# Two sets of operand sums change engines in the score rounds of a cross-attention kernel

## The chip, the cores and the metric

The kernel runs on one core of a Trainium2 chip. The metric is the device time of one launch in microseconds (us). PE is TensorE, DVE is VectorE, ACT is ScalarE, POOL is GpSimd, SP is SyncE (here it only issues DMA transfers).

## The reference

```python
def reference(x, ctx, mask, Wq, Wk, Wv, Wo, gamma, beta, gate):   # x 8x1024x1024, ctx 8x64x1024
    a = layer_norm(ctx, gamma, beta)
    Q = split_heads(x @ Wq.T)            # 16 heads of 64
    K = split_heads(a @ Wk.T)
    V = split_heads(a @ Wv.T)
    s = where(mask, Q @ K.T * 64 ** -0.5, -inf)   # 8 x 16 x 1024 x 64
    out = merge_heads(softmax(s) @ V) @ Wo.T
    return x + tanh(gate) * out
```

Everything is float32.

## The kernel before

Since a batch has only 64 keys, Wq and K are multiplied first: for every batch b the kernel builds M[b], a 1024x1024 matrix (model dimension by 16 heads times 64 keys), in scratch DRAM, so that all scores of the batch are x[b] times M[b]. That is the first stage (about 186 us). The second stage, the score rounds, does these products; the third, the output rounds, does softmax, the product with V, and the product with Wo.

A score round n (0 to 15) is one half batch, 512 rows of x, against M[n // 2], 1024x1024. The product is split once by a seven-product scheme in the manner of Strassen and Winograd: the left operand A (the transposed x) is cut into four quadrants, the right operand B (M) into four quadrants, and seven products of sums of quadrants, P1, P5, P6, P3, P7, P2, P4 in this order, give the result. A *step* s is one such product: n = s // 7, k = s % 7. Steps 0 to 111 are score rounds, 112 to 223 output rounds. A step is two groups of 12 matmuls (every float32 operand is split into a high and a low float32r part, and high*low, low*high, high*high are added), plus one small mask matmul for each group of P1.

Around each step:

- **Sums of A.** P5, P6, P3 and P7 have a sum or difference of A quadrants on the left; P1, P2, P4 take a quadrant as it is. `sum_a(n, k)` makes such a sum, 128x1024 elements, from `xq` (the loaded quadrants of x) into `a_sum` (two buffers). Before the change it is a POOL instruction (line 552), and the semaphore `sum_made` counts them: 4 a round, 64 in the score rounds.
- **Split of A.** `split_a_hi(s)` is an ACT cast into `a_ring` (L656), `split_a_lo(s)` the DVE subtraction behind it (L849). PE's step s waits for the latter (`a_lo_made`). `a_ring` has two slots, so the cast for step s+1 starts when step s-1 is done (`item_done`).
- **Sums of B.** Once a batch (every 14 steps) the seven B operands in `parts` are refilled for the next batch, two pieces (q = 0 to 13) for each product, while the second round of the batch is running: `refill_step` puts pieces q at steps 8 to 19 counted from the first step of the batch's round pair. `sum_b(rnd, k)` makes the four B sums in place in `b_raw` (three 128x2048 buffers), for P5, P6, P7, P4, after pieces 1, 3, 5 and 11. Before the change it is a DVE instruction (L883), 128x2048 elements, counted by `t_made`: 4 a batch, 32 in all. The cast of the next piece (`split_b_hi`, ACT, L680) waits for it; the DVE subtraction `split_b_lo` (L862) follows the cast.
- **Results.** `copy_out` (ACT, L691) copies the first product into an output quadrant from PSUM, `add_out` (DVE, L905) adds the others.

Each engine takes its instructions strictly in the order in which the program issues them; semaphores alone join the engines. DVE's order in step s is: `add_out` of step s-1, `split_a_lo(s+1)`, the refill pieces of step s with their B sum, and at the ninth step of every batch the small mask instruction (L844). POOL has nothing else to do in these rounds, so it does each A sum as soon as its inputs and its buffer are free.

Of the kernel before, what the change touches and what calls it, by code (L numbers as in the profile page):

```python
# [5 lines left out]
ALU = mybir.AluOpType  # L6
# [13 lines left out]
def xattn_kernel(nc, x, x_t, ctx_x, mask, wq_b, wk_t, wv_t, wo_t, gamma, beta, gate, out):  # L20
    rows, D = x.shape
    B, S = mask.shape
# [20 lines left out]
    with ExitStack() as ctx:  # L43
# [20 lines left out]
        b_raw = at("b_raw", 112, [P, 3, HC, HD])  # L64
        a_sum = at("a_sum", 136, [P, 2, HC, 2, P])
# [73 lines left out]
        m_stored = sems("m_stored", 3)  # L139
# [80 lines left out]
        def a_quad(n, r, half):  # L220
            return x_pair(2 * n + half)[:, :, :, r, :]

        def a_source(n, k):
            if k in A_QUAD:
                return a_quad(n, *A_QUAD[k])
            return a_sum[:, A_SUM[k]]

        def wait_quad(eng, n, half):
            if n < ROUNDS:
                y = 2 * n + half  # L230
                eng.wait_ge(x_in[y % 3], 16 * (y // 3 + 1))
            else:
                eng.wait_ge(o_made, NC * (n - ROUNDS) + HC * (half + 1))
# [14 lines left out]
        def refills(s):  # L248
            return [(rnd, q) for rnd in range(B + 1) for q in range(14) if refill_step(rnd, q) == s]
# [259 lines left out]
        @block.gpsimd  # L509
        def _(pool):  # L510
            nc.gpsimd.memset(ident[:], 0.0).then_inc(ident_zero, 1)
            pool.wait_ge(ident_zero, 1)
            nc.gpsimd.affine_select(out=ident[:], in_=ident[:], compare_op=ALU.not_equal, fill=1.0, base=0,
                                    pattern=[[-1, P]], channel_multiplier=1).then_inc(ident_made, 1)
            nc.gpsimd.memset(neg_half[:], -0.5).then_inc(ident_zero, 1)
            nc.gpsimd.memset(ones_row[:].bitcast(F32), 0.0).then_inc(rows_zeroed, 1)
            pool.wait_ge(ident_zero, 2)
            for i in range(CT):
                pool.wait_ge(var_added, i + 1)
                nc.gpsimd.tensor_tensor(rstd[:, i:i + 1], var_eps[:, i:i + 1], neg_half[:], ALU.pow  # L520
                                        ).then_inc(rstd_made, 1)
            pool.wait_ge(rows_zeroed, 1)
            nc.gpsimd.memset(ones_row[0:1, :].bitcast(F32), 1.0).then_inc(rows_zeroed, 1)
            for w in range(ITEMS):
                hi, lo = w_ring[:, w % 6, 0, :], w_ring[:, w % 6, 1, :]
                pool.wait_ge(w_hi_made, w + 1)
                nc.gpsimd.tensor_tensor(lo, w_raw[:, w % 4, :], hi.bitcast(F32), ALU.subtract).then_inc(w_lo_made, 1)

            def sum_a(n, k):
                if k == P5:  # L530
                    wait_quad(pool, n, 0)
                    wait_quad(pool, n, 1)
                    if n > 0:
                        pool.wait_ge(a_lo_made, 7 * (n - 1) + P3 + 1)
                    else:
                        pool.wait_ge(m_stored[2], 16 * 5)
                        pool.wait_ge(m_first_stored[0], 16)
                    one, two, op = a_quad(n, 1, 0), a_quad(n, 1, 1), ALU.add
                elif k == P6:
                    pool.wait_ge(sum_made, 4 * n + 1)  # L540
                    if n > 0:
                        pool.wait_ge(a_lo_made, 7 * (n - 1) + P7 + 1)
                    one, two, op = a_sum[:, 0], a_quad(n, 0, 0), ALU.subtract
                elif k == P3:
                    pool.wait_ge(sum_made, 4 * n + 2)
                    pool.wait_ge(a_lo_made, 7 * n + P5 + 1)
                    one, two, op = a_quad(n, 0, 1), a_sum[:, 1], ALU.subtract
                else:
                    pool.wait_ge(sum_made, 4 * n + 3)
                    pool.wait_ge(a_lo_made, 7 * n + P6 + 1)  # L550
                    one, two, op = a_quad(n, 0, 0), a_quad(n, 1, 0), ALU.subtract
                nc.gpsimd.tensor_tensor(a_sum[:, A_SUM[k]], one, two, op).then_inc(sum_made, 1)  # L552

            def normalise(u):
                pr = probs[:, u % 4, :].rearrange("p (g s) -> p g s", s=S)
                rec = row_rec[:, u % 2, :].unsqueeze(2).to_broadcast([P, 8, S])
                pool.wait_ge(rec_done, u + 1)
                nc.gpsimd.tensor_tensor(pr, pr, rec, ALU.mult).then_inc(probs_done, 1)  # L558

            sum_a(0, P5)  # L560
            sum_a(0, P6)
            for s in range(STEPS):
                n, k = s // 7, s % 7
                if k == P5:
                    sum_a(n, P3)
                if k == P6:
                    sum_a(n, P7)
                if s == 102:
                    pool.wait_ge(t_made, 4 * B)
                    nc.gpsimd.memset(v_diag[:].bitcast(F32), 0.0).then_inc(v_zeroed, 1)  # L570
                for u in units(2 * s, SUM):
                    normalise(u)
                for u in units(2 * s + 1, SUM):
                    normalise(u)
                if k == P4 and n + 1 < 2 * ROUNDS:
                    sum_a(n + 1, P5)
                    sum_a(n + 1, P6)

# [162 lines left out]
        def _(dve):  # L741
# [104 lines left out]
            def split_a_lo(s):  # L846
                n, k = s // 7, s % 7
                dve.wait_ge(a_hi_made, s + 1)
                nc.vector.tensor_tensor(a_ring[:, s % 2, 1], a_source(n, k), a_ring[:, s % 2, 0].bitcast(F32),  # L849
                                        ALU.subtract).then_inc(a_lo_made, 1)  # L850
# [11 lines left out]
                nc.vector.tensor_tensor(parts[:, k, 1, c:c + 2, :], b_raw[:, B_HOME[k], c:c + 2, :],  # L862
                                        parts[:, k, 0, c:c + 2, :].bitcast(F32), ALU.subtract).then_inc(b_lo_made, 1)

            def sum_b(rnd, k):
                r0, r1, r2 = b_raw[:, 0], b_raw[:, 1], b_raw[:, 2]
                if k == P5:
                    dve.wait_ge(b_in[1], 16 * (rnd + 1))
                    dve.wait_ge(b_lo_made, 14 * rnd + 2)
                    to, one, two = r0, r1, r0  # L870
                elif k == P6:
                    dve.wait_ge(b_in[2], 32 * rnd + 16)
                    dve.wait_ge(b_lo_made, 14 * rnd + 4)
                    to, one, two = r0, r2, r0
                elif k == P7:
                    dve.wait_ge(t_made, 4 * rnd + 1)
                    to, one, two = r1, r2, r1
                else:
                    dve.wait_ge(b_in[2], 32 * rnd + 32)
                    dve.wait_ge(t_made, 4 * rnd + 2)  # L880
                    dve.wait_ge(b_lo_made, 14 * rnd + 12)
                    to, one, two = r2, r2, r0
                nc.vector.tensor_tensor(to, one, two, ALU.subtract).then_inc(t_made, 1)  # L883

            def refill(s):
                for rnd, q in refills(s):
                    split_b_lo(rnd, q)
                    if rnd < B and q in (1, 3, 5, 11):
                        sum_b(rnd, {1: P5, 3: P6, 5: P7, 11: P4}[q])

            def bank_pair(n, k):
                return banks[:, 4:6, :] if k in ON_F else banks[:, 2 * (n % 2):2 * (n % 2) + 2, :]
# [37 lines left out]
            split_a_lo(0)  # L930
            for i in range(CT):
                split_v_lo(1, i)
            for s in range(STEPS):
                rnd = s // 14 + 1
                if s > 0:
                    add_out((s - 1) // 7, (s - 1) % 7)
                if s + 1 < STEPS:
                    split_a_lo(s + 1)
                if s < 104:
                    refill(s)  # L940
                for z in (2 * s, 2 * s + 1):
# [203 lines left out]
```

## Time and profile before

| | us |
|---|---|
| median of 3 runs | 1643.02 (1642.58 to 1645.21) |
| the profiled execution: its own time | 1641.88 |
| its span, first to last instruction | 1640.1 |
| PE busy | 1554.1 (95%) |
| DVE busy | 1173.1 (72%) |
| ACT busy | 860.6 (52%) |
| POOL busy | 536.4 (33%) |

The busy times are sums over the span of one profiled execution. Matmuls overlap in PE's pipeline (one is recorded with 0.39 us and the next starts 0.23 us later), so PE's progress is read from start to start.

### The profile page before, as it was taken

Reading aid. Unit: us, or ns where it says so; the run is one execution under the profiler, and the core shown is the slowest. Engines: PE = TensorE matmul, PEld = TensorE weight load, DVE = VectorE, ACT = ScalarE, POOL = GpSimd, SP = SyncE. Lnnn points to the kernel's source line nnn. Section 1 sums busy time; section 2 is a strip of 40 time slices with the busy share of each in tenths; the row PEclk is TensorE's granted clock in tenths of the full one; section 3 lists DMA queues with packets and bytes.
Section 4 is the critical chain, followed back from the end, with each engine's and each line's share of the span. In section 5 each row is a group of like instructions: output and inputs, shape, how many; then the busy total and the mean of one; then the engine's idle time right before and its main releaser. Section 6 shows DMA issues by size and latency. Waiting matters only on the chain.

```text
span 1640.1 us, 19978 instructions
## 1 busy us (share of the span) xinstructions
PE 1554.1 (95%) x7104; PEld 1254.7 (77%) x7104; DVE 1173.1 (72%) x1216; ACT 860.6 (52%) x1822; POOL 536.4 (33%) x294
## 2 busy tenths in 40 slices
PE   6998799999999999999988999999999999999998
PEld 5755577777777778777766788888888888888887
DVE  8534678686868696968767877777777777777763
ACT  3444344343444444444666766666666666666641
POOL 6322122323232323222323333343433334443331
PEclk9999899999999999999999999999999999999999
DMA  6999862636363635353446544344444434454422
GB/s 232 320 361 377 292 226 103 213 106 210 105 215 106 213 106 202 125 183 128 156 125 183 180 131 135 121 134 137 156 152 132 138 120 133 139 155 149 139 80 90
DMA packets 203841, 275.05 MB, mean 168 GB/s; under 512 B 26464, under 2 KB 92128, under 8 KB 203744
## 3 DMA queue, kind: packets, MB, share of 16 engines
q1 hardware_dynamic: 203744, 273.79, 50.5%
q8 instruction: 57, 0.93, 0.2%
q14 instruction: 40, 0.33, 0.1%
HBM read 164.70 MB, written 109.05 MB: 167 GB/s over the span
## 4 chain that ended last, share of the span: by engine, by line
PE 69%; DVE 14%; issue 6%; DMA 6%; ACT 4%; POOL 0%; SPq 0%; ACTq 0%; DVEq 0%; POOLq 0%
PE banks L966 22%; PE banks L968 21%; PE banks L967 21%; DVE a_ring L849 4%; DVE parts L862 3%; PE banks L1092 3%; DVE c_out L905 2%; DMA w_raw<-wq_b 2%; ACT parts L680 1%; PE banks L1002 1%; DMA w_raw<-wv_t 1%; ACT c_out L691 1%; DMA m_scratch<-m_stage 1%; DVE mask_mov L844 1%; DVE b_raw L883 1%
## 5 line engine op out<-in xcount | busy, mean ns | idle before, releaser
L966 PE MATMUL banks<-parts,a_ring 128*128 128x512 f32 x1792 | 717.6, 400 | 30.7 <-DVE a_ring L849 18.2
L968 PE MATMUL banks<-parts,a_ring 128*128 128x512 f32 x1792 | 703.4, 393 | 0.0
L967 PE MATMUL banks<-parts,a_ring 128*128 128x512 f32 x1792 | 702.8, 392 | 0.0
L966 PEld LDWEIGHTS banks<-parts,a_ring 128*128 128x128 f32 x1792 | 339.7, 190 | 106.0 <-DVE a_ring L849 25.2
L968 PEld LDWEIGHTS banks<-parts,a_ring 128*128 128x128 f32 x1792 | 339.1, 189 | 73.5
L967 PEld LDWEIGHTS banks<-parts,a_ring 128*128 128x128 f32 x1792 | 339.9, 190 | 67.2
L558 POOL TENSOR_TENSOR probs<-probs,row_rec 128x512 f32<-128x512 f32 x128 | 133.8, 1045 | 497.0 <-DVE row_rec L919 497.0
L697 ACT ACTIVATE probs<-probs,neg_max 128x64 f32<-128x64 f32 x1024 | 259.1, 341 | 49.2 <-DVE neg_max L910 49.2
L905 DVE TENSOR_TENSOR c_out<-banks,c_out 128x1024 f32<-128x1024 f32 x160 | 195.1, 1219 | 119.0 <-PE banks L968 114.4
L849 DVE TENSOR_TENSOR a_ring<-a_sum,a_ring 128x1024 fp32r<-128x1024 f32 x128 | 188.4, 1472 | 113.7 <-ACT a_ring L656 112.5
L656 ACT CAST a_ring<-a_sum 128x1024 fp32r<-128x1024 f32 x128 | 134.0, 1047 | 211.6 <-PE banks L968 202.3
L552 POOL TENSOR_TENSOR a_sum<-xq 128x1024 f32<-128x1024 f32 x64 | 167.8, 2622 | 210.0 <-DMA xq<-x_t 105.1
L862 DVE TENSOR_TENSOR parts<-b_raw,parts 128x1024 fp32r<-128x1024 f32 x112 | 186.1, 1676 | 29.4 <-ACT parts L680 29.0
L656 ACT CAST a_ring<-xq 128x1024 fp32r<-128x1024 f32 x96 | 100.5, 1046 | 159.6 <-PE banks L968 159.6
L706 ACT CAST p_parts<-banks 128x512 fp32r<-128x512 f32 x128 | 74.6, 583 | 168.6 <-PE banks L968 114.0
L552 POOL TENSOR_TENSOR a_sum<-xq,a_sum 128x1024 f32<-128x1024 f32 x32 | 77.5, 2423 | 247.2 <-DVE a_ring L849 247.2
L680 ACT CAST parts<-b_raw 128x1024 fp32r<-128x1024 f32 x112 | 115.2, 1047 | 60.2 <-DVE b_raw L883 54.4
L923 DVE TENSOR_TENSOR p_parts<-banks,p_parts 128x512 fp32r<-128x512 f32 x128 | 86.9, 679 | 80.6 <-ACT p_parts L706 80.6
L849 DVE TENSOR_TENSOR a_ring<-xq,a_ring 128x1024 fp32r<-128x1024 f32 x96 | 123.9, 1291 | 2.4 <-ACT a_ring L656 2.4
L915 DVE TENSOR_REDUCE row_sum<-probs 128x8 f32<-128x512 f32 x128 | 87.2, 681 | 19.1 <-ACT probs L697 17.8
L883 DVE TENSOR_TENSOR b_raw<-b_raw 128x2048 f32<-128x2048 f32 x32 | 96.9, 3028 | 3.1 <-DVE parts L862 0.5
L552 POOL TENSOR_TENSOR a_sum<-a_sum,xq 128x1024 f32<-128x1024 f32 x32 | 93.6, 2924 | 11.4 <-DVE a_ring L849 9.4
(74 smaller groups left out, 1266.7 us busy)
## 6 DMA issues: line engine op xcount, KB each, us to landing
xq<-x_t SPq DMA_DIRECT2D x32, 1024.0 KB, 6.8
b_raw<-m_scratch SPq DMA_DIRECT2D x32, 1024.0 KB, 6.3
s_scratch<-c_out SPq DMA_DIRECT2D x64, 512.0 KB, 3.1
probs<-s_scratch SPq DMA_DIRECT2D x128, 256.0 KB, 3.1
c_out<-x SPq DMA_DIRECT2D x64, 512.0 KB, 4.7
out<-c_out SPq DMA_DIRECT2D x64, 512.0 KB, 3.1
m_scratch<-m_stage SPq DMA_DIRECT2D x14, 2048.0 KB, 15.6
w_raw<-wk_t SPq DMA_DIRECT2D x8, 512.0 KB, 7.6
```

The lines of the kernel that those rows point to most:

```text
L552: nc.gpsimd.tensor_tensor(a_sum[:, A_SUM[k]], one, two, op).then_inc(sum_made, 1)
L558: nc.gpsimd.tensor_tensor(pr, pr, rec, ALU.mult).then_inc(probs_done, 1)
L656: nc.scalar.copy(a_ring[:, s % 2, 0], a_source(n, k)).then_inc(a_hi_made, 1)
L680: nc.scalar.copy(parts[:, k, 0, c:c + 2, :], b_raw[:, B_HOME[k], c:c + 2, :]).then_inc(b_hi_made, 1)
L697: last = nc.scalar.activation(probs[:, u % 4, cols], probs[:, u % 4, cols], ACT.Exp, bias=neg_max[:, u % 2, g:g + 1])
L849: nc.vector.tensor_tensor(a_ring[:, s % 2, 1], a_source(n, k), a_ring[:, s % 2, 0].bitcast(F32), ALU.subtract).then_inc(a_lo_made, 1)
L862: nc.vector.tensor_tensor(parts[:, k, 1, c:c + 2, :], b_raw[:, B_HOME[k], c:c + 2, :], parts[:, k, 0, c:c + 2, :].bitcast(F32), ALU.subtra ...
L883: nc.vector.tensor_tensor(to, one, two, ALU.subtract).then_inc(t_made, 1)
L905: nc.vector.tensor_tensor(c_out[:, q], bank_pair(n, k), c_out[:, q], ALU.add).then_inc(added, 1)
L966: pe.matmul(to, wl, mh, start=first, stop=False, skip_group_check=joined)
L967: pe.matmul(to, wh, ml, start=False, stop=False, skip_group_check=joined)
L968: return pe.matmul(to, wh, mh, start=False, stop=last, skip_group_check=joined)
```

## The change

In the score rounds the A sums are issued on VectorE, one at a time inside its steps, and all B sums on GpSimd. In the output rounds (n >= 16) nothing changes: A sums stay on GpSimd. The instructions keep their shapes and operands, and the semaphores their counts; each wait moves with its instruction.

```diff
@@ GpSimd @@
-            sum_a(0, P5)
-            sum_a(0, P6)
+            def refill_sums(s):
+                for rnd, q in refills(s):
+                    if rnd < B and q in (1, 3, 5, 11):
+                        sum_b(rnd, {1: P5, 3: P6, 5: P7, 11: P4}[q])
+
+            refill_sums(-1)
             for s in range(STEPS):
                 n, k = s // 7, s % 7
-                if k == P5:
+                refill_sums(s)
+                if k == P5 and n >= ROUNDS:
                     sum_a(n, P3)
-                if k == P6:
+                if k == P6 and n >= ROUNDS:
                     sum_a(n, P7)
...
-                if k == P4 and n + 1 < 2 * ROUNDS:
+                if k == P4 and ROUNDS <= n + 1 < 2 * ROUNDS:
                     sum_a(n + 1, P5)
                     sum_a(n + 1, P6)
@@ VectorE @@
             def refill(s):
                 for rnd, q in refills(s):
                     split_b_lo(rnd, q)
-                    if rnd < B and q in (1, 3, 5, 11):
-                        sum_b(rnd, {1: P5, 3: P6, 5: P7, 11: P4}[q])
...
+            sum_a(0, P5)
             for s in range(STEPS):
...
                 if s + 1 < STEPS:
                     split_a_lo(s + 1)
+                if k == P1 and n < ROUNDS:
+                    sum_a(n, P6)
+                if k == P5 and n < ROUNDS:
+                    sum_a(n, P3)
+                if k == P6 and n < ROUNDS:
+                    sum_a(n, P7)
+                if k == P4 and n + 1 < ROUNDS:
+                    sum_a(n + 1, P5)
                 if s < 104:
                     refill(s)
```

The GpSimd form of `sum_b` and its waits, which the prediction speaks of:

```python
            def sum_b(rnd, k):
                r0, r1, r2 = b_raw[:, 0], b_raw[:, 1], b_raw[:, 2]
                if k == P5:
                    pool.wait_ge(b_in[1], 16 * (rnd + 1))
                    pool.wait_ge(b_lo_made, 14 * rnd + 2)
                    to, one, two = r0, r1, r0
                elif k == P6:
                    pool.wait_ge(b_in[2], 32 * rnd + 16)
                    pool.wait_ge(b_lo_made, 14 * rnd + 4)
                    to, one, two = r0, r2, r0
                elif k == P7:
                    pool.wait_ge(t_made, 4 * rnd + 1)
                    to, one, two = r1, r2, r1
                else:
                    pool.wait_ge(b_in[2], 32 * rnd + 32)
                    pool.wait_ge(t_made, 4 * rnd + 2)
                    pool.wait_ge(b_lo_made, 14 * rnd + 12)
                    to, one, two = r2, r2, r0
                nc.gpsimd.tensor_tensor(to, one, two, ALU.subtract).then_inc(t_made, 1)
```

VectorE's order from the ninth step of the first round pair on, before (`a_ring` is the split of A, `parts` the split of B, `b_raw` a B sum, `c_out` an `add_out`):

```order
L862 TENSOR_TENSOR parts<-b_raw,parts 128x1024 x2
L883 TENSOR_TENSOR b_raw<-b_raw 128x2048
L849 TENSOR_TENSOR a_ring<-a_sum,a_ring 128x1024
L862 TENSOR_TENSOR parts<-b_raw,parts 128x1024
L844 TENSOR_SCALAR mask_mov<-mask_u 1x512
L849 TENSOR_TENSOR a_ring<-a_sum,a_ring 128x1024
L862 TENSOR_TENSOR parts<-b_raw,parts 128x1024
L883 TENSOR_TENSOR b_raw<-b_raw 128x2048
L905 TENSOR_TENSOR c_out<-banks,c_out 128x1024
L849 TENSOR_TENSOR a_ring<-xq,a_ring 128x1024
```

and after, at the same place (line numbers of the changed kernel: L910 is a sum of A, L875 the split of A, L888 the split of B, L930 an `add_out`):

```order
L910 TENSOR_TENSOR a_sum<-xq,a_sum 128x1024
L888 TENSOR_TENSOR parts<-b_raw,parts 128x1024 x2
L875 TENSOR_TENSOR a_ring<-a_sum,a_ring 128x1024
L910 TENSOR_TENSOR a_sum<-xq 128x1024
L888 TENSOR_TENSOR parts<-b_raw,parts 128x1024
L870 TENSOR_SCALAR mask_mov<-mask_u 1x512
L875 TENSOR_TENSOR a_ring<-a_sum,a_ring 128x1024
L888 TENSOR_TENSOR parts<-b_raw,parts 128x1024
L930 TENSOR_TENSOR c_out<-banks,c_out 128x1024
L875 TENSOR_TENSOR a_ring<-xq,a_ring 128x1024
```

The two 128x2048 B sums are gone from between the splits, and two 128x1024 A sums (for P3 and P7 of the round) stand there.

GpSimd's order from the end of its weight splits on, before:

```order
L527 TENSOR_TENSOR w_ring<-w_raw,w_ring 128x1024 x24
L552 TENSOR_TENSOR a_sum<-xq 128x1024
L552 TENSOR_TENSOR a_sum<-a_sum,xq 128x1024
L552 TENSOR_TENSOR a_sum<-xq,a_sum 128x1024
L552 TENSOR_TENSOR a_sum<-xq 128x1024 x2
```

and after:

```order
L536 TENSOR_TENSOR w_ring<-w_raw,w_ring 128x1024 x24
L573 TENSOR_TENSOR b_raw<-b_raw 128x2048 x32
L596 MEMSET v_diag 128x2048
L579 TENSOR_TENSOR probs<-probs,row_rec 128x512 x11
L553 TENSOR_TENSOR a_sum<-xq 128x1024
```

All 32 B sums stand in a row on GpSimd, with nothing between them but their waits, and the first A sum that GpSimd makes is that of the first output round.

## Rows read from the trace of the kernel before

**Rows 1.** The page, part 1: busy time by engine, share of the span, instructions
```profile
PE 1554.1 (95%) x7104; PEld 1254.7 (77%) x7104; DVE 1173.1 (72%) x1216; ACT 860.6 (52%) x1822; POOL 536.4 (33%) x294
```
**Rows 2.** Windows: start:end, length, busy of each engine (count), clock, DMA share, GB/s
```profile
186.00:249.00 63.00, 53.22 (x195) 42.15 (x196) 45.72 (x31) 23.52 (x24) 19.67 (x7) 0.84 0.68 228
249.00:768.00 519.00, 500.27 (x2187) 408.56 (x2186) 403.63 (x255) 229.53 (x233) 149.69 (x51) 1.00 0.45 153
```
**Rows 3.** Waits of PE, 249 to 768 us: who, us in total, times, longest
```profile
PE banks L966 <- DVE a_ring L849: 18.2, 12, 2.3
PE banks L966 <- issue: 0.6, 1, 0.6
```
**Rows 4.** Timeline of PE: start, duration, instruction [idle before]
```profile
313.01 0.50 PE L966 MATMUL banks<-parts,a_ring 128*128 128x512 f32 x1 [1.19 <-DVE a_ring L849]
...
593.46 0.39 PE L968 MATMUL banks<-parts,a_ring 128*128 128x512 f32 x1
595.43 0.50 PE L966 MATMUL banks<-parts,a_ring 128*128 128x512 f32 x1 [1.58 <-DVE a_ring L849]
...
599.66 0.39 PE L966 MATMUL banks<-parts,a_ring 128*128 128x512 f32 x1
...
606.46 0.39 PE L1079 MATMUL banks<-mask_mov,ones_row 128*128 128x512 f32 x1
```
**Rows 5.** Timeline of DVE, steps 64 to 68
```profile
573.08 1.23 DVE L849 TENSOR_TENSOR a_ring<-a_sum,a_ring 128x1024 fp32r<-128x1024 f32 x1 [4.67 <-ACT a_ring L656]
574.94 4.13 DVE L862 TENSOR_TENSOR parts<-b_raw,parts 128x1024 fp32r<-128x1024 f32 x2 [0.63 <-ACT parts L680]
...
587.49 1.21 DVE L862 TENSOR_TENSOR parts<-b_raw,parts 128x1024 fp32r<-128x1024 f32 x1
588.80 4.31 DVE L883 TENSOR_TENSOR b_raw<-b_raw 128x2048 f32<-128x2048 f32 x1
593.03 1.21 DVE L905 TENSOR_TENSOR c_out<-banks,c_out 128x1024 f32<-128x1024 f32 x1
594.16 1.21 DVE L849 TENSOR_TENSOR a_ring<-xq,a_ring 128x1024 fp32r<-128x1024 f32 x1
```
**Rows 6.** Timeline of POOL in the same steps
```profile
574.45 2.40 POOL L552 TENSOR_TENSOR a_sum<-xq 128x1024 f32<-128x1024 f32 x1 [3.51 <-DVE a_ring L849]
...
587.70 3.26 POOL L552 TENSOR_TENSOR a_sum<-a_sum,xq 128x1024 f32<-128x1024 f32 x1 [1.55 <-DVE a_ring L849]
```
**Rows 7.** Timeline of ACT in the same steps
```profile
577.44 1.05 ACT L656 CAST a_ring<-a_sum 128x1024 fp32r<-128x1024 f32 x1 [1.58 <-PE banks L968]
```
**Rows 8.** Sources L552, L558, L511: count, ns min/median/max, first and last start, shape
```profile
L552 POOL TENSOR_TENSOR a_sum<-xq,a_sum x32: 2377/2398/3192, 196.9 to 1600.0; 128x1024 f32<-128x1024 f32 x32
L558 POOL TENSOR_TENSOR probs<-probs,row_rec x128: 1042/1045/1049, 797.2 to 1577.7; 128x512 f32<-128x512 f32 x128
L511 POOL MEMSET ident<- x1: 205/205/205, 0.7 to 0.7; 128x128 f32 x1
```
**Rows 9.** Timeline of DVE and POOL in the first stage
```profile
22.32 14.83 DVE L767 TENSOR_TENSOR a_parts<-a_scaled_t,a_parts 128x512 fp32r<-128x512 f32 x7
...
24.45 10.95 POOL L527 TENSOR_TENSOR w_ring<-w_raw,w_ring 128x1024 fp32r<-128x1024 f32 x4 [0.29 <-ACT w_ring L589]
```
**Rows 10.** Timeline of POOL, PE and DVE in the first score round
```profile
190.78 2.38 POOL L552 TENSOR_TENSOR a_sum<-xq 128x1024 f32<-128x1024 f32 x1 [32.73 <-DMA xq<-x_t]
...
201.24 0.77 PE L966 MATMUL banks<-parts,a_ring 128*128 128x512 f32 x1 [5.78 <-issue]
...
224.24 0.77 PE L966 MATMUL banks<-parts,a_ring 128*128 128x512 f32 x1 [3.53 <-issue]
...
194.28 2.45 DVE L849 TENSOR_TENSOR a_ring<-a_sum,a_ring 128x1024 fp32r<-128x1024 f32 x1 [5.29 <-ACT a_ring L656]
196.65 4.49 DVE L862 TENSOR_TENSOR parts<-b_raw,parts 128x1024 fp32r<-128x1024 f32 x2
```
**Rows 11.** Timeline of DVE where the score rounds end, last B sum
```profile
789.42 2.29 DVE L883 TENSOR_TENSOR b_raw<-b_raw 128x2048 f32<-128x2048 f32 x1
```

More of the change, by code:

```diff
@@ L226, in a_source, with sum_operands @@
             return a_sum[:, A_SUM[k]]
+        def sum_operands(n, k):
+            if k == P5:
+                return a_quad(n, 1, 0), a_quad(n, 1, 1), ALU.add
+            if k == P6:
+                return a_sum[:, 0], a_quad(n, 0, 0), ALU.subtract
+            if k == P3:
+                return a_quad(n, 0, 1), a_sum[:, 1], ALU.subtract
+            return a_quad(n, 0, 0), a_quad(n, 1, 0), ALU.subtract
         def wait_quad(eng, n, half):
@@ L532, in sum_a @@
                     wait_quad(pool, n, 1)
[L533 to L538, printed above, removed]
+                    pool.wait_ge(sum_made, 4 * n)
+                    pool.wait_ge(a_lo_made, 7 * (n - 1) + P3 + 1)
                 elif k == P6:
                     pool.wait_ge(sum_made, 4 * n + 1)
-                    if n > 0:
-                        pool.wait_ge(a_lo_made, 7 * (n - 1) + P7 + 1)
-                    one, two, op = a_sum[:, 0], a_quad(n, 0, 0), ALU.subtract
+                    pool.wait_ge(a_lo_made, 7 * (n - 1) + P7 + 1)
                 elif k == P3:
@@ L546, in sum_a @@
                     pool.wait_ge(a_lo_made, 7 * n + P5 + 1)
-                    one, two, op = a_quad(n, 0, 1), a_sum[:, 1], ALU.subtract
                 else:
@@ L550, in sum_a, with sum_b @@
                     pool.wait_ge(a_lo_made, 7 * n + P6 + 1)
-                    one, two, op = a_quad(n, 0, 0), a_quad(n, 1, 0), ALU.subtract
-                nc.gpsimd.tensor_tensor(a_sum[:, A_SUM[k]], one, two, op).then_inc(sum_made, 1)
+                nc.gpsimd.tensor_tensor(a_sum[:, A_SUM[k]], *sum_operands(n, k)).then_inc(sum_made, 1)
+            def sum_b(rnd, k):
+                r0, r1, r2 = b_raw[:, 0], b_raw[:, 1], b_raw[:, 2]
+                if k == P5:
+                    pool.wait_ge(b_in[1], 16 * (rnd + 1))
+                    pool.wait_ge(b_lo_made, 14 * rnd + 2)
+                    to, one, two = r0, r1, r0
+                elif k == P6:
+                    pool.wait_ge(b_in[2], 32 * rnd + 16)
+                    pool.wait_ge(b_lo_made, 14 * rnd + 4)
+                    to, one, two = r0, r2, r0
+                elif k == P7:
+                    pool.wait_ge(t_made, 4 * rnd + 1)
+                    to, one, two = r1, r2, r1
+                else:
+                    pool.wait_ge(b_in[2], 32 * rnd + 32)
+                    pool.wait_ge(t_made, 4 * rnd + 2)
+                    pool.wait_ge(b_lo_made, 14 * rnd + 12)
+                    to, one, two = r2, r2, r0
+                nc.gpsimd.tensor_tensor(to, one, two, ALU.subtract).then_inc(t_made, 1)
             def normalise(u):
@@ L863, in split_b_lo, with sum_a @@
                                         parts[:, k, 0, c:c + 2, :].bitcast(F32), ALU.subtract).then_inc(b_lo_made, 1)
-            def sum_b(rnd, k):
-                r0, r1, r2 = b_raw[:, 0], b_raw[:, 1], b_raw[:, 2]
+            def sum_a(n, k):
                 if k == P5:
-                    dve.wait_ge(b_in[1], 16 * (rnd + 1))
-                    dve.wait_ge(b_lo_made, 14 * rnd + 2)
-                    to, one, two = r0, r1, r0
-                elif k == P6:
[L872 to L877, printed above, removed]
-                else:
[L879 to L883, printed above, removed]
+                    wait_quad(dve, n, 0)
+                    wait_quad(dve, n, 1)
+                    if n > 0:
+                        dve.wait_ge(a_lo_made, 7 * (n - 1) + P3 + 1)
+                    else:
+                        dve.wait_ge(m_stored[2], 16 * 5)
+                        dve.wait_ge(m_first_stored[0], 16)
+                elif k == P6:
+                    dve.wait_ge(sum_made, 4 * n + 1)
+                    if n > 0:
+                        dve.wait_ge(a_lo_made, 7 * (n - 1) + P7 + 1)
+                elif k == P3:
+                    dve.wait_ge(sum_made, 4 * n + 2)
+                    dve.wait_ge(a_lo_made, 7 * n + P5 + 1)
+                else:
+                    dve.wait_ge(sum_made, 4 * n + 3)
+                    dve.wait_ge(a_lo_made, 7 * n + P6 + 1)
+                nc.vector.tensor_tensor(a_sum[:, A_SUM[k]], *sum_operands(n, k)).then_inc(sum_made, 1)
             def refill(s):
@@ L932, in _ @@
                 split_v_lo(1, i)
+            sum_a(0, P5)
             for s in range(STEPS):
-                rnd = s // 14 + 1
+                rnd, n, k = s // 14 + 1, s // 7, s % 7
                 if s > 0:
```

## The prediction

> **What bounds the kernel now.** I read the page's busy times first: PE 95%, DVE 72%, POOL 33% [rows 1]. An engine at 33% that takes work from one at 72% sounds like relief, but PE is the bound, so the second view was the windows: what does PE lose, and where? From 249 to 768 us (90 steps, from the ninth step of batch 0 to step 98) the clock is at its upper level, 1.00, throughout [rows 2]. The timeline gives PE's own pace: from 599.66 to 606.46 us lie 30 matmuls, 0.227 us each [rows 4], so a step of 24 is 5.44 us. The waits of that stretch then name the loss: 12 waits of 18.2 us for the DVE split of A, L849, and one of 0.6 us put down to issue [rows 3]. A wait costs a little more than its entry. From the last matmul at 593.46 to the next at 595.43 are 1.97 us where 0.23 is usual, so 1.74 is lost for an entry of 1.58; and from 595.43 to 599.66 are 18 matmuls in 4.23 us instead of 4.08, 0.15 more. That is 0.31 on top of each entry: 18.8 + 13 x 0.31 = 22.8 us in seven periods of 14 steps. All else in these rounds is hidden behind PE.
>
> Then the timelines of DVE and POOL around one stall. DVE's B sum at 588.80 took 4.31 us where the same instruction takes 2.29 when POOL is idle [rows 5, 11]. POOL's A sum started at 587.70 and ended at 590.96 [rows 6]; 593.11 less 2.29 is 590.82. So DVE did nothing until POOL was done. POOL in turn took 3.26 us instead of 2.40, since DVE's split ran until 588.70: both stand still for each other, whole instructions long, whenever both DVE operands are in SBUF. The `add_out` behind it, with PSUM as one operand, kept its 1.21. Behind the long B sum stand `add_out` and the split of A for step 68, which ended at 595.37; PE went on at 595.43. That is one stall of each period. The other kind (1.19, at 313.01 us) is behind the P4 sum, in the same way [rows 4].
>
> **The price of the moved instructions.** A sums on DVE: 128x1024, two SBUF operands, like the split of A: one each 1.14 us (593.03 to 594.16), 1.21 to 1.23 recorded [rows 5]. B sums on POOL: 128x2048 is not in the trace. The nearest row is the 1024 form of the same operation, 2.40 us median; twice that less one fixed part, for which a whole POOL memset of 0.205 us stands: 4.57 [rows 8]. Call it X. From below: a POOL multiply of 512 elements takes 1.045, four of them 4.18. From above: the step from 512 to 1024 is 1.355, so 2.40 + 2 x 1.355 = 5.11. I take 4.57 and keep both ends. Over a batch the pair is then held for 8 x 1.14 + 4 x 4.57 = 27.4 us of sums instead of 8 x 2.40 + 4 x 2.29 = 28.4: no relief in total. What counts is that the longest single block for DVE grows from 2.40 to 4.57.
>
> The Trainium skill, GPSIMD Engine Reference, section 3.1, gives 4497 ns for a `tensor_tensor` add of 2048 float32 on GpSimd and 2293 ns on VectorE; the second agrees with the 2.29 here. With its 4.50 the sum below would come out 1.5 us lower.
>
> **One period after the change, in the times of steps 64 to 69.** Step 66 is due at 593.69 - 2 x 5.44 = 582.81.
>
> Step 64: the split of A starts at 573.08 as before [rows 5], the A sum for P3 at 574.22, the splits of B pieces 0 and 1 at 575.36 and 576.50, the last ending at 577.71 (before: 579.07, since POOL's A sum was in the way). POOL started 0.14 behind such an end (574.31 to 574.45) [rows 5, 6], so the P5 sum of B runs from 577.85 to 577.85 + X. The split of A for step 66 is ready at 578.49, when its cast ends [rows 7], and must wait: a blocked split ends 1.09 behind POOL's end (its 1.23 less the 0.14 by which 590.82 lies ahead of 590.96), PE follows 0.06 later. Step 66 starts at 579.00 + X = 583.57: **stall 0.76**, which was not there before.
>
> Step 66: after the A sum for P7, piece 2, the mask, the split of A and piece 3, DVE reaches about 588.5; the P6 sum of B runs 588.6 to 593.2. The split of A for step 68 is blocked until then and ends at 594.27; due is 583.57 + 0.15 + 10.88 = 594.60. No stall, but only 0.27 of slack; as three blocked waits lie in it, I put 0.15 a period for it.
>
> Step 68: the P7 sum of B waits for nothing but the first sum, so it stands ready behind P6 and takes the pair when that split ends: until 594.27 - 0.14 + 4.57 = 598.70. Piece 4 ends at 599.79, `add_out` and the split of A for step 69 follow 1.14 apart: 602.07, PE at 602.13. Due is 594.60 + 5.44 = 600.04: **stall 2.09**, in the place of the 1.74.
>
> The P4 sum comes at the end of step 73; POOL's two A sums that crowded it are gone, and the split of A that it blocks (for step 75) has 0.6 us to spare by the same chain, so the stall of the second kind goes.
>
> Sum: 0.76 + 2.09 + 2 x 0.15 = 3.15 a period, x7 = 22.1 against 22.8: **-0.7**; slack term 7 x 0.15: **+1.0**. Each X lies once in the first stall and twice more in the second, so one us of X is 21 us of time.
>
> **The first round** [rows 2, 10]. The A sum waits for a load until 190.78. On DVE it takes 1.2 instead of 2.38, and neither the split (2.45) nor the two pieces (4.49) behind it are blocked: 192.0, cast 193.1, split 194.3, A sum 195.5, pieces 197.8. Step 1 starts at 197.9 instead of 201.24, 3.3 earlier. Then P6 and P7 of B, 2 X = 9.1 on POOL, stand in front of step 2's pieces, ending near 211.3, where two DVE sums of 2.29 stood: 2 later than before. PE idles some 5 us there, and after such gaps it starts at the lower of its two levels, 1.2 GHz of 2.4 (0.77 recorded where 0.39 is usual; granted clock 0.84 over the window: 0.16 x 63 = 10 us, about 3.4 for each of three restarts). The restart of 224.24, with 3.53 idle, goes in exchange. I come out even at step 4: **0**, with 3 either way.
>
> **The end.** The last P4 sum of B, 2.29 at 789.42 [rows 11], is X on POOL: ACT's cast behind it, and the first exponentials of the output rounds, start 2.3 later; part of that is slack: **+1.0** (0 to 2.3). Covered at nothing: the later A sum for P7 (it releases a load of x some 7 us later, which is needed 20 us after), and DVE's A sums in steps without a B sum, where ACT's cast leaves DVE idle (4.67) [rows 5].
>
> Total +1.3: 1643.2 for the profiled execution (1641.88 before), 1644.3 for the median (1643.02). It can't be told from no change, which I take as within 0.2%, 3.3 us.
>
> **Rivals.**
> - *X is dearer.* At 4.80, strictly twice 2.40, the periods cost 7 x 3 x 0.23 = 4.8 more: 1649; at 5.11, 1656. It decides from X = 4.67, where the total passes +3.3. For it: nothing in the trace shows a fixed part on a subtract. Chance 0.22.
> - *POOL keeps the pair between P6 and P7*, which have no wait between them: the split for step 68 ends 4.4 later, the stall of 2.09 becomes one of 4.1 with the restart a step earlier, and step 69 goes on 5.44 behind it: 2.4 more a period, 1661. Against it: in the first stage four back-to-back POOL instructions took 10.95 us instead of 4 x 2.40 = 9.6 while DVE had seven splits to do, and only 1.75 us lie between their ends (35.40 and 37.15): most of the splits got in between [rows 9]. Chance 0.06.
> - *X is cheaper* or the blocked splits end earlier than I chain them: below X = 4.35 the total is under -3.3; at 4.18 it is 1.3 - 8.2, 1636. For it: the 512-element row. Chance 0.17.
> - *The first round keeps its gain*: PE stays at the upper clock over the second gap (up to 3.4 less) and step 2 is not later: 1639. Against it: both gaps of this length fell. Chance 0.10.
> - The advice of the Trainium skill, Perfetto Trace Analysis, that moving work between VectorE and GpSimd "might not help" as they share a port, would be no change; the row with 4.31 agrees.
>
> **How the numbers follow.** The forecast has 0.45, with 1641 to 1647.5 as its own range. Slower by over 0.2%: 0.22 + 0.06 and a little of the forecast's edge, 0.29. Faster: 0.17 + 0.10 less edges, 0.25. Same: 0.46. The range leaves out the two ends of X and POOL keeping the pair: 1637.5 to 1653.
>
> **What would show it.** POOL's B sum at 4.5 to 4.6 us when alone. In every period PE stalls before steps 66 and 69 (counted as here), 0.8 and 2.1, each released by the split of A, and none at step 75. DVE's splits of A recorded with up to 5 us beside a POOL B sum. PE's first matmul of step 1 near 198, one at half pace near 211. Wrong would be: stalls before step 68; two B sums of POOL with no DVE instruction ended between them; DVE instructions not stretched by POOL's B sums.

## The result, and the profile after

The changed kernel takes 1656.81 us (median of 4 runs, 1654.07 to 1657.62), the kernel before 1644.12 us beside it (4 runs, 1642.58 to 1645.26). The ratio is 1.0075, 95% interval 1.0057 to 1.0092: slower by 0.75%, above the upper end of the forecast's range. The profiled execution took 1657.14 us with a span of 1655.4, against 1641.88 and 1640.1: 15.3 us more to explain. The kernel before was timed 26 times more beside the experiments, on two other occasions, and spread further there, from 1641.91 to 1651.56; the slowest of those runs still lies below the fastest of the changed kernel.

Page, part 1, of the changed kernel (busy time, share, instructions):

```profile
PE 1564.0 (94%) x7104; PEld 1260.3 (76%) x7104; DVE 1179.9 (71%) x1248; ACT 861.5 (52%) x1822; POOL 509.0 (31%) x262
```

Against [rows 1] nearly nothing is to be seen there except one thing: PE executes the same 7104 matmuls and is busy for 9.9 us longer. Matmuls that wait for an operand are not busy, so some matmuls ran longer. (DVE's time rose by 6.8 us and POOL's fell by 27.4, since the instructions changed places.) The windows say where. They are cut at the first matmul of steps 0, 8, 98 and 112 (start:end, length, busy of PE, PEld, DVE, ACT, POOL with counts, granted clock, DMA share, GB/s), changed kernel. A step of P1 begins with a mask matmul, and step 0 is counted from the one behind it:

```profile
185.70:250.20 64.50, 52.15 (x196) 41.23 (x195) 46.60 (x32) 23.75 (x25) 19.27 (x4) 0.86 0.68 231
250.20:780.10 529.90, 509.56 (x2187) 414.27 (x2186) 409.05 (x279) 230.38 (x233) 131.17 (x27) 0.98 0.44 150
780.10:883.30 103.20, 92.88 (x414) 75.04 (x413) 71.90 (x90) 66.41 (x155) 19.17 (x14) 0.97 0.50 156
```

| stretch | before | after | difference |
|---|---|---|---|
| first stage, to step 0 | 187.0 | 185.7 | -1.3 |
| step 0 to 8 (first round) | 62.3 | 64.5 | +2.2 |
| step 8 to 98 (seven periods) | 519.0 | 529.9 | **+10.9** |
| step 98 to 112 | 100.9 | 103.2 | +2.3 |
| step 112 to the last matmul | 765.9 | 767.1 | +1.2 |

The seven periods hold most of it, and there the granted clock is 0.98 where [rows 2] have 1.00. PE's waits there (who, us in total, times, longest):

```profile
PE banks L1000 <- DVE a_ring L875: 20.3, 14, 2.1
```

[Rows 3] had 18.2 in 12 for the same split of A (L849 then, L875 now) and 0.6 for issue. The waits alone therefore grew by 1.5 us. The rest is in PE's timeline around one of these stalls, before step 69 (start, duration, instruction, idle before it and its releaser):

```profile
606.86 0.39 PE L1002 MATMUL banks<-parts,a_ring 128*128 128x512 f32 x1
609.33 0.50 PE L1000 MATMUL banks<-parts,a_ring 128*128 128x512 f32 x1 [2.08 <-DVE a_ring L875]
609.67 0.40 PE L1001 MATMUL banks<-parts,a_ring 128*128 128x512 f32 x1
609.90 0.59 PE L1002 MATMUL banks<-parts,a_ring 128*128 128x512 f32 x1
610.29 0.63 PE L1000 MATMUL banks<-parts,a_ring 128*128 128x512 f32 x1
...
612.86 0.62 PE L1000 MATMUL banks<-parts,a_ring 128*128 128x512 f32 x1
613.28 0.43 PE L1001 MATMUL banks<-parts,a_ring 128*128 128x512 f32 x1
```

From 606.86 to 609.33 are 2.47 us where 0.23 is usual: a stall of 2.24. Then, from 609.90 on, the matmuls start 0.43 apart instead of 0.23. That is PE's lower clock, 1.2 GHz, and the windows around another such stall (step 13, restart at 281.07) give it outright: 1.00, then 0.50, then 1.00.

```profile
278.80:282.20 3.40, 1.32 (x6) 0.95 (x6) 3.40 (x4) 2.95 (x3) 0.00 (x0) 1.00 0.40 154
282.30:285.60 3.30, 3.30 (x9) 2.53 (x8) 3.30 (x4) 0.00 (x0) 0.00 (x0) 0.50 0.42 158
285.70:343.00 57.30, 57.30 (x254) 47.45 (x254) 38.37 (x29) 24.57 (x25) 8.84 (x2) 1.00 0.52 174
```

Eight matmuls at 0.43 instead of 0.23 cost 1.6 us. It happened behind five of the seven stalls of this kind. Behind the last one (restart at 774.25) and the one at 528.45, of the same length, it did not:

```profile
525.96 0.39 PE L1002 MATMUL banks<-parts,a_ring 128*128 128x512 f32 x1
528.45 0.50 PE L1000 MATMUL banks<-parts,a_ring 128*128 128x512 f32 x1 [2.10 <-DVE a_ring L875]
528.78 0.40 PE L1001 MATMUL banks<-parts,a_ring 128*128 128x512 f32 x1
529.01 0.40 PE L1002 MATMUL banks<-parts,a_ring 128*128 128x512 f32 x1
529.25 0.40 PE L1000 MATMUL banks<-parts,a_ring 128*128 128x512 f32 x1
```

From the restart at 528.45 to the next are 80.88 us; from a restart with the drop to the next are 82.46. So five times 1.58, 7.9 us, of the +10.9 are clock, and about 3.0 are stalls.

What makes the stalls is as forecast. DVE and POOL of the changed kernel around them:

```profile
585.25 5.03 DVE L875 TENSOR_TENSOR a_ring<-a_sum,a_ring 128x1024 fp32r<-128x1024 f32 x1 [0.81 <-ACT a_ring L682]
590.20 1.21 DVE L910 TENSOR_TENSOR a_sum<-xq 128x1024 f32<-128x1024 f32 x1
...
597.25 4.21 DVE L875 TENSOR_TENSOR a_ring<-xq,a_ring 128x1024 fp32r<-128x1024 f32 x1
601.55 5.46 DVE L888 TENSOR_TENSOR parts<-b_raw,parts 128x1024 fp32r<-128x1024 f32 x1
606.94 1.21 DVE L930 TENSOR_TENSOR c_out<-banks,c_out 128x1024 f32<-128x1024 f32 x1
608.07 1.21 DVE L875 TENSOR_TENSOR a_ring<-xq,a_ring 128x1024 fp32r<-128x1024 f32 x1
```
```profile
584.58 4.61 POOL L573 TENSOR_TENSOR b_raw<-b_raw 128x2048 f32<-128x2048 f32 x1 [24.56 <-DVE parts L888]
595.76 10.16 POOL L573 TENSOR_TENSOR b_raw<-b_raw 128x2048 f32<-128x2048 f32 x2 [6.58 <-DVE parts L888]
```

POOL's P5 sum (584.58, 4.61 us) holds up DVE's split of A until 590.28: stall before step 66. The P6 and P7 sums follow each other within 10.16 us, more than twice 4.61, because one DVE split (597.25, 4.21) gets in between them; the piece at 601.55 then waits for the second, and behind it come `add_out` and the split of A that PE waits for at 609.33.

The first round, PE of the changed kernel:

```profile
198.82 0.77 PE L1000 MATMUL banks<-parts,a_ring 128*128 128x512 f32 x1 [5.21 <-issue]
...
212.09 0.77 PE L1000 MATMUL banks<-parts,a_ring 128*128 128x512 f32 x1 [5.25 <-issue]
...
238.77 0.47 PE L1000 MATMUL banks<-parts,a_ring 128*128 128x512 f32 x1 [1.83 <-issue]
```

Step 1 starts 2.4 us earlier than in the trace of before (201.24, [rows 10]), step 2 2.7 later, step 3 5.1 later and step 8 0.9 later, although step 0 starts 1.3 earlier. Idle times of 5.2 in front of steps 1 and 2 and 1.8 in front of step 6 stand where 5.8 and 3.5 stood.

### The profile page after: what moved, and what is told of

It reads as the page before. It is cut to its first block, busy times and chain, and to the rows that moved or that the text cites. A ratio compares the mean times of both kernels' runs of the same rounds, so it can differ in the third digit from the quotient of the medians.

```text
span 1655.4 us, 19994 instructions
## 1 busy us (share of the span) xinstructions
PE 1564.0 (94%) x7104; PEld 1260.3 (76%) x7104; DVE 1179.9 (71%) x1248; ACT 861.5 (52%) x1822; POOL 509.0 (31%) x262
## 4 chain that ended last, share of the span: by engine, by line
PE 69%; DVE 10%; issue 7%; DMA 6%; ACT 4%; POOL 2%; SPq 0%; ACTq 0%; DVEq 0%; POOLq 0%
PE banks L1000 22%; PE banks L1002 21%; PE banks L1001 21%; PE banks L1126 3%; DVE a_ring L875 3%; POOL b_raw L573 2%; DMA w_raw<-wq_b 2%; DMA w_raw<-wv_t 2%; DVE c_out L930 2%; PE banks L1036 1%; ACT a_ring L682 1%; DVE a_parts L793 1%; ACT parts L706 1%; ACT probs L723 1%; DMA m_scratch<-m_stage 1%
## 5 line engine op out<-in xcount | busy, mean ns | idle before, releaser
L573 POOL TENSOR_TENSOR b_raw<-b_raw 128x2048 f32<-128x2048 f32 x32 | 156.7, 4909 | 490.2 <-DVE parts L888 490.2
L875 DVE TENSOR_TENSOR a_ring<-a_sum,a_ring 128x1024 fp32r<-128x1024 f32 x128 | 213.2, 1666 | 118.5 <-ACT a_ring L682 117.5
L930 DVE TENSOR_TENSOR c_out<-banks,c_out 128x1024 f32<-128x1024 f32 x160 | 195.4, 1221 | 132.9 <-PE banks L1002 126.9
L888 DVE TENSOR_TENSOR parts<-b_raw,parts 128x1024 fp32r<-128x1024 f32 x112 | 168.5, 1519 | 15.0 <-ACT parts L706 13.5
L875 DVE TENSOR_TENSOR a_ring<-xq,a_ring 128x1024 fp32r<-128x1024 f32 x96 | 158.0, 1646 | 2.2 <-ACT a_ring L682 2.2
L1126 PE MATMUL banks<-ident,probs 128*128 128x128 f32 x512 | 78.0, 275 | 15.4 <-DVE p_parts L948 14.6
L1126 PEld LDWEIGHTS banks<-ident,probs 128*128 128x128 f32 x512 | 62.6, 141 | 37.2 <-issue 19.3
L852 DVE COPY m_stage<-banks 128x512 f32<-128x512 f32 x64 | 43.7, 690 | 59.6 <-PE banks L1036 46.8
## 6 DMA issues: line engine op xcount, KB each, us to landing
m_scratch<-m_stage SPq DMA_DIRECT2D x14, 2048.0 KB, 15.8
```

What stands on the lines that cost most here:

```text
L573: nc.gpsimd.tensor_tensor(to, one, two, ALU.subtract).then_inc(t_made, 1)
L930: nc.vector.tensor_tensor(c_out[:, q], bank_pair(n, k), c_out[:, q], ALU.add).then_inc(added, 1)
L1126: m = pe.transpose(banks[:, 6, cols], probs[:, u % 4, cols], ident[:])
```

## Experiments

All start from the changed kernel unless said otherwise. The kernel before was run beside them: 1643.86 us for the first four (13 runs, 1641.91 to 1650.14), 1646.71 for the last three (13 runs on another chip, 1643.47 to 1651.56), so ratios to it are what compares across the two sets, and differences of a few us between sets are not settled by them. Stretches of the traces are compared beside the times. The diffs are cut; where a sum is made in several instructions, the counts of `t_made` in the waits follow.

### The P7 sum of B as 1536 and 512 columns

Does the clock follow the length of the stall? The last block in front of step 69 is made shorter; nothing else in the work changes.

```diff
+                if k == P7:
+                    for c, e in ((0, 3), (3, 4)):
+                        nc.gpsimd.tensor_tensor(to[:, c:e, :], one[:, c:e, :], two[:, c:e, :], ALU.subtract
+                                                ).then_inc(t_made, 1)
+                    return
...
```

> As the changed kernel, but GpSimd makes the P7 sum of B in two instructions, 1536 columns and then 512, with the same work in all. The block in front of the split of B piece 4 shrinks from 4.6 us to 3.5, and the stall before the last step of each period (2.24 us in the changed kernel) to about 1.1. Clock theory (five of seven 2.24 us stalls were followed by 3.4 us at half clock, 1.6 us lost each, and that is most of what the prediction missed): the half-clock stretches go too, 7 x 1.15 + 7.9 = 16 us less than the changed kernel's 1656.8: 1641. Rival (the loss is the stalls themselves and the pair being held; the clock stretches are incidental): 8 us less, 1649.

Measured: 1641.22 us (1639.67 to 1643.05, 10 runs), ratio 0.9983 (0.9972 to 0.9995). PE in front of step 69, and the window from step 8 to 98:

```profile
597.98 0.39 PE L1007 MATMUL banks<-parts,a_ring 128*128 128x512 f32 x1
599.35 0.50 PE L1005 MATMUL banks<-parts,a_ring 128*128 128x512 f32 x1 [0.98 <-DVE a_ring L880]
599.68 0.39 PE L1006 MATMUL banks<-parts,a_ring 128*128 128x512 f32 x1
```
```profile
250.50:764.60 514.10, 501.49 (x2186) 408.47 (x2185) 401.51 (x279) 230.42 (x233) 139.13 (x34) 1.00 0.45 154
```

The stall is 1.14 instead of 2.24, in all seven periods, and no half clock follows any. The stretch is 15.8 us shorter than in the changed kernel: 7 x 1.10 = 7.7 of stalls and the 7.9 of the clock. The clock theory said 1641, the rival 1649. The 7.9 us have no wait of their own in the trace of the changed kernel: they are matmuls at 0.43 us behind the longer stall, and they are gone with it.

### The P7 sum of B held back

```diff
                 elif k == P7:
                     pool.wait_ge(t_made, 4 * rnd + 1)
+                    if rnd > 0:
+                        pool.wait_ge(a_lo_made, 14 * rnd)
```

> As the changed kernel, but in batches 1 to 7 GpSimd's P7 sum of B also waits until VectorE has made the split of A for the last step of the round, so that it is not in the way before that step. The 2.24 us stall goes altogether; the 0.97 us one stays. Chaining the rows of the changed kernel gives 16.8 us less in stalls and restarts. Clock theory: the 7.9 us of half clock go as well, 1632. Rival (clock incidental): 1640. If the pair, held as long in all as before, only moves the stall elsewhere: 1650 or more.

Measured: 1630.48 us (1630.0 to 1631.57, 4 runs), ratio 0.9921 (0.9904 to 0.9937), as the clock theory had it (1632; the rival 1640).

```profile
250.00:755.10 505.10, 499.40 (x2186) 409.01 (x2185) 392.70 (x277) 230.38 (x233) 130.63 (x27) 1.00 0.46 157
```
```profile
PE banks L1002 <- DVE a_ring L877: 5.7, 7, 0.8
```

Of the two stalls of a period only the one in front of step 66 is left, seven waits. The stretch is 24.8 us shorter than in the changed kernel; 7 x (2.24 + 0.15) + 7.9 = 24.6. POOL does the same work in the same number of instructions (27, 130.6 us): of these 24.8 us it is when the block comes that decides, not how much POOL works.

### All sums of B in two halves

```diff
-                nc.gpsimd.tensor_tensor(to, one, two, ALU.subtract).then_inc(t_made, 1)
+                for c in (0, 2):
+                    nc.gpsimd.tensor_tensor(to[:, c:c + 2, :], one[:, c:c + 2, :], two[:, c:c + 2, :], ALU.subtract
+                                            ).then_inc(t_made, 1)
```

> As the changed kernel, but every B sum on GpSimd is made in two instructions of 1024 columns, so that VectorE can get in between. If what costs is the length of one block (4.6 us against 2.4): stalls shrink by some 7 us and the half-clock stretches within the periods go (7.9): 1642. If what costs is the total time that GpSimd holds the pair (the same here, or a little more by a second fixed part): no change, 1657.

Measured: 1652.27 us (1651.44 to 1653.94, 4 runs), ratio 1.0052 (1.0037 to 1.0067): neither number. PE's waits, the window from step 8 to 98, and DVE and POOL around step 69:

```profile
PE banks L1002 <- DVE a_ring L877: 17.6, 7, 2.8
```
```profile
252.90:776.20 523.30, 505.69 (x2187) 414.89 (x2186) 370.57 (x279) 228.81 (x233) 154.51 (x54) 0.98 0.45 151
```
```profile
594.85 11.42 POOL L574 TENSOR_TENSOR b_raw<-b_raw 128x1024 f32<-128x1024 f32 x4 [5.43 <-DVE parts L890]
```
```profile
601.75 2.28 DVE L890 TENSOR_TENSOR parts<-b_raw,parts 128x1024 fp32r<-128x1024 f32 x1 [3.42 <-ACT parts L708]
603.96 1.21 DVE L932 TENSOR_TENSOR c_out<-banks,c_out 128x1024 f32<-128x1024 f32 x1
605.09 2.26 DVE L877 TENSOR_TENSOR a_ring<-xq,a_ring 128x1024 fp32r<-128x1024 f32 x1
```

The stall in front of step 66 is gone, as expected: a half blocks for less than the slack there. The one in front of step 69 now loses 2.6 to 3.0 us, where the changed kernel has 2.24, and the clock is 0.98 again, low behind five of the seven. P6 and P7 are now four halves in a row, ACT's cast waits for both halves of a sum (DVE stood idle for 3.42 us for it), and of the two P7 halves one is in front of the piece (2.28 us recorded) and the other in front of the split of A (2.26). So the chain to that split is as long as ever. Shorter blocks helped where a single block was the cause, not where the sum itself was waited for.

### Sums of A on DVE alone

One of the two moves by itself: `sum_b` goes back to DVE's `refill`, and POOL has nothing to do in the score rounds.

```diff
             def refill(s):
                 for rnd, q in refills(s):
                     split_b_lo(rnd, q)
+                    if rnd < B and q in (1, 3, 5, 11):
+                        sum_b(rnd, {1: P5, 3: P6, 5: P7, 11: P4}[q])
```

> One half of the change alone: the A sums of the score rounds on VectorE as in the changed kernel, the B sums on VectorE as before; GpSimd does nothing in the score rounds. VectorE gets 64 x 1.14 = 73 us of work more than before, but no GpSimd instruction blocks it. Theory (all stalls of both kernels are blocks behind GpSimd): all stalls before and in the periods go (22.8 us) and the first round gets some 7 us shorter: 1614 to 1618. Rival (VectorE, at 72 to 78% in these rounds, is too full for both): stalls stay or grow, 1644 or more.

Measured: **1615.32 us** (1613.71 to 1616.38, 4 runs), ratio 0.9825 (0.9811 to 0.984), faster than both kernels by more than 28 us, as the theory had it (1614 to 1618). The window from step 8 to 98, and a B sum:

```profile
243.00:738.30 495.30, 495.30 (x2187) 410.12 (x2186) 378.70 (x306) 230.46 (x233) 0.00 (x0) 1.00 0.47 160
```
```profile
557.36 2.29 DVE L903 TENSOR_TENSOR b_raw<-b_raw 128x2048 f32<-128x2048 f32 x1
```

PE is busy for the whole stretch; the trace has no wait of PE in it. 495.3 is 23.7 less than before and 34.6 less than changed. So the stalls of [rows 3] too hang on POOL's work in these rounds: with POOL idle none is left, though DVE does all the sums beside the splits. DVE is even recorded as less busy (378.7 us for 306 instructions, 403.6 for 255 in [rows 2]), since time in which it is held up counts as busy.

### Sums of B on POOL alone

The other move by itself, from the kernel before: `sum_b` goes to POOL, behind that step's sum of A for P3 or P7 and ahead of the two for the next round; all sums of A stay there.

```diff
             for s in range(STEPS):
...
+                refill_sums(s)
                 if s == 102:
```

> The other half of the change alone: B sums on GpSimd, A sums on GpSimd too, as before; VectorE makes no sums in the score rounds. In each step GpSimd's A sum stands ahead of its B sum. Theory (what costs is GpSimd holding the pair, and its own queue): the pair is held by GpSimd for 8 x 2.4 + 4 x 4.6 = 37.6 us a batch, and A sums now queue behind B sums; well over both kernels, 1690 to 1705. Rival (the harm of the change is only the long B block, and the A sums are neutral on either engine): like the changed kernel, 1657.

Measured: 1694.85 us (1694.42 to 1696.24, 4 runs), ratio 1.0284 (1.0261 to 1.0308), as the theory had it (1690 to 1705; the rival 1657).

```profile
260.00:818.00 558.00, 515.07 (x2186) 416.42 (x2185) 429.00 (x228) 229.61 (x233) 284.04 (x78) 0.98 0.42 142
```
```profile
PE banks L971 <- DVE a_ring L876: 32.5, 21, 3.1
PE banks L971 <- issue: 10.4, 6, 1.7
```

The change is two moves of opposite sign: the sums of A to DVE take 1.75% off, the sums of B to POOL add 2.84%. Added up they would be +1.1%, and +0.75% was measured; the two need not add up, since here the sums of B also share POOL's queue with those of A.

### Sums of B of batch 0 back on DVE

```diff
             def refill_sums(s):
                 for rnd, q in refills(s):
-                    if rnd < B and q in (1, 3, 5, 11):
+                    if 0 < rnd < B and q in (1, 3, 5, 11):
```

(and `if rnd == 0` with the same `sum_b` on DVE.)

> As the changed kernel, but the four B sums of batch 0 are made by VectorE as before; batches 1 to 7 stay on GpSimd. It shows what the first round costs in the changed kernel: there PE stopped twice for 5.4 us (steps 1 and 2) and started again at half clock both times. With the A-only kernel's first round (step 8 at 243.0 us against 250.2) 7 us less: 1650. If the first round is bound by the loads and not by the GpSimd blocks: 1656.

Measured: 1652.76 us (1647.62 to 1653.61, 10 runs), ratio 1.0023 (1.0008 to 1.0039). Windows of steps 0 to 8 and 8 to 98:

```profile
190.60:246.40 55.80, 49.53 (x197) 39.34 (x196) 42.46 (x36) 23.69 (x24) 0.00 (x0) 0.92 0.76 256
246.40:776.40 530.00, 509.50 (x2187) 414.28 (x2186) 410.10 (x279) 230.48 (x233) 131.30 (x27) 0.98 0.44 149
```

The first round is 8.7 us shorter than in the changed kernel (64.5); the periods are as they were. The median is only 4.1 us lower, as step 0 came 4.9 us later in this trace (190.6 against 185.7). The ratio is lower by 0.0052, 8.6 us, but that difference is known to 4 us either way only, so it is the trace that shows the 8.7. So the +2.2 of this round is a gain of 6.5 from the sums of A (62.3 to 55.8) and a loss of 8.7 from the sums of B. In these ten runs one more thing is seen: the two fastest, 1647.62 and 1648.47, have a mean granted clock of 0.988 and 0.987, seven of the others 0.981 to 0.983 and 1652.1 to 1653.6, and one 0.982 at 1649.6. The program is the same in all. This trace has the same seven stalls as that of the changed kernel, and again the clock fell behind five, but not the same five: here the second (restart at 359.76) and not the third (442.19). After the restarts, windows:

```profile
359.90:363.30 3.40, 3.40 (x9) 2.63 (x10) 3.40 (x4) 0.79 (x1) 0.00 (x0) 0.50 0.41 156
442.20:445.60 3.40, 3.40 (x15) 2.80 (x16) 3.40 (x4) 0.95 (x1) 0.00 (x0) 1.00 0.42 158
```

So which of the stalls the clock follows is not fixed by their place in the period or by their length. That how many it follows varies from run to run fits the mean clocks; only one of the ten runs has a trace.

### The sums of A of the output rounds on DVE too

From the version with the sums of A alone; POOL then keeps only the softmax's multiplications.

```diff
-                if k == P1 and n < ROUNDS:
+                if k == P1:
...
-                if k == P4 and n + 1 < ROUNDS:
+                if k == P4 and n + 1 < 2 * ROUNDS:
```

> The A-only kernel taken further: the A sums of the output rounds on VectorE as well, so that GpSimd makes no sums at all, only the softmax normalisation. In the output rounds VectorE has 575 of 805 us to do and is waited for by exponentials and the P splits, not blocked by GpSimd much. Theory (a move to VectorE pays where a block behind GpSimd is what PE waits for, and there alone): 5 to 10 us more than the A-only kernel's 1615: 1620 to 1625. Rival (less GpSimd is better everywhere): under 1612.

Measured: 1621.62 us (1620.36 to 1621.83, 4 runs), ratio 0.9837 (0.9815 to 0.9859). By the ratios it is 2 us slower than A alone, by the times 6.3, and the intervals overlap. The profiled spans differ by 7.4 us, of which 3.5 lie in the first stage and 0.9 in the first round, which the edit does not touch. Behind step 98 are 3.1: 1.5 up to step 112 and 1.6 from there to the last matmul (769.9 us against 768.3). So it brings nothing, and the 5 to 10 us expected are not seen; these traces show about 3.

## Why the prediction was wrong

- **Price of a B sum on POOL.** Forecast 4.57, measured 4.60 to 4.62 alone. Right; the two rivals with another X fall, since 0.04 x 21 is 0.8 us. The Trainium skill, GPSIMD Engine Reference, section 3.1, has 4497 ns for an add of 2048; the measurement, 2.4 to 2.7% above it, decides.
- **Who stands still for whom.** Right in each place: the split of A for step 66 (5.03 us recorded), a DVE split between P6 and P7, so POOL does not keep the pair, a hitch of 0.17 in front of step 68 and none at step 75. The Trainium skill, SBUF — State Buffer, section "Who interferes with whom", says that whichever instruction is first keeps the shared ports to its end and the other waits; the trace agrees, with 4.61 in front and 5.03 behind.
- **Size of the stalls.** 0.76 was 0.97, 2.09 was 2.24. With the hitch and two restarts that is 3.38 + 0.30 = 3.68 a period, 25.8 us in seven against 22.8 before: +3.0 where the terms -0.7 and +1.0 stood. Under-sized by 2.7 us; the 21 X of the sum explain 0.8 of that.
- **The step that failed: the clock.** The periods were summed "in the times of steps 64 to 69", from [rows 2] with their 1.00. There was no term for what the stall does to the clock behind it, although such a term was charged in the first round, for idle times of 3.53 us and more. The stall grew from 1.74 to 2.24, and where none of the twelve stalls of before was followed by the lower clock (seven of 1.74, four of 1.35, one of 2.50), five of seven now were: **7.9 us**. The cut to 1.14 took it away, with 7.7 us of the stalls themselves (0.9983 in place of 1.0075). This is more than half of the miss of 14 us. The stall of 2.50 in the trace of before, and the window behind it with its clock of 1.00:

```profile
713.81 0.39 PE L968 MATMUL banks<-parts,a_ring 128*128 128x512 f32 x1
716.54 0.50 PE L966 MATMUL banks<-parts,a_ring 128*128 128x512 f32 x1 [2.33 <-DVE a_ring L849]
```
```profile
716.50:720.00 3.50, 3.46 (x15) 2.90 (x16) 3.50 (x4) 0.75 (x1) 0.00 (x0) 1.00 1.01 291
```

  The Trainium skill, TensorE: Matmul & The Clock Gate, section "HAM oscillation — how this bites in real kernels", describes a kernel in which a wait repeated every iteration drops the clock every time and the transition is paid each time. Its waits, about 3 to 5 us, are longer than these. The traces agree in five periods of seven, with 2.24 us each; I had not applied it to a stall that short.
- **First round.** Forecast 0 with 3 either way, measured +2.2. Step 1 came at 198.8 (forecast 197.9) and step 2's restart at half pace at 212.1 (forecast 211.3). "Even at step 4" was wrong: step 4 starts 1.6 us later than before, and the idle 1.8 before step 6 was not foreseen. The single moves give +8.7 and -6.5.
- **End.** Forecast +1.0, measured +2.3, just at the bound named. The late cast delays the first transposition:

```profile
809.99 0.39 PE L1002 MATMUL banks<-parts,a_ring 128*128 128x512 f32 x1
811.03 0.66 PE L1126 MATMUL banks<-ident,probs 128*128 128x128 f32 x4 [0.65 <-POOL probs L579]
```

  That is 0.81 of it; a stall in front of the second half of step 107 grew from 4.79 to 5.74, which is nearly another 1.0. This second part is not shown to come from the late sum: with POOL idle (sums of A on DVE alone) the same stall is 5.61.
- **Not foreseen, not explained.** +1.2 in the output rounds, which the change does not touch; the version with the sums of A alone has +2.4 there. No experiment looked into it. The first stage was 1.3 us shorter, also untouched by the change; with step 0 at 190.6 and 190.8 in two experiments, it varies by more than that.
- **Sum.** Stalls +3.0, clock +7.9, first round +2.2, end +2.3, output rounds +1.2, first stage -1.3: +15.3.
- **The view I did not take.** The forecast compared the new arrangement with the old one, both with two engines on one pair of ports, and found the held time nearly equal (27.4 and 28.4 us a batch). True, and it hid that one of the two moves alone ends the contest. From step 8 to 98 the version with POOL idle takes 495.3 us; with POOL's 130.6 us of work at the best place tried it takes 505.1, at the place of the change 529.9. POOL's share of 31% says neither.

Open: why two of seven equal stalls, and the single one of 2.50 before, were not followed by the lower clock (that other ones of the seven escape in another trace says that it varies, not why); the +1.2 of the output rounds; the longer stall in step 107.

## What to carry to other kernels

Where the trace shows two engines standing still for each other for whole instructions, as DVE and POOL do here, cost the arrangement in which one of them does all of the work before you exchange work between them. Here the version with POOL idle is the fastest measured (1615.32 us, 1.75% under the kernel before). And where PE is the bound, give each repeated stall a second term, the granted clock behind it. If the stall grows past the lengths that the trace shows to be harmless again and again (1.74 here, seven times; a single one of 2.50 proved nothing), let the range reach from nothing to that term in every period: 7 x 1.6 us here.

## What the runs showed of the hardware

- Idle time of 2.24 us in front of full matmul work was followed by about 3.4 us at clock 0.50 in five cases of seven, each costing 1.6 us; stalls of 1.74 (seven, before) and of 1.14 (seven, with the shortened block) never were. Nor was the one stall of 2.50 in the trace of before. In the steady stretch (step 8 to 98) of the other traces: again five of seven stalls of 2.24 to 2.26 (sums of B of batch 0 on DVE), five of seven of 2.6 to 3.0 (halves), six of seven of 3.3 (sums of B alone), and none of seven of 1.9 there. Length alone does not decide.
- POOL's 128x2048 float32 subtraction takes 4.60 to 4.62 us alone and 128x1024 takes 2.40. An estimate from these two sizes: 2.2 for each 1024 elements and a fixed part of 0.2.
- Two POOL instructions back to back do not shut DVE out: one waiting DVE instruction gets in between (10.16 us for two of 4.61, with a DVE split ended between them).
- A DVE instruction held up by one of POOL is recorded as busy all the while, so busy time can fall when work is added: DVE 403.6 us for 255 instructions beside POOL, 378.7 for 306 with POOL idle.
